# A fused decoder in float32 on one core: rotary attention's bank reads go ahead of the block turnings, and the second group's query weight sums go ahead of the last two rotations

## The reference

```python
def _L1_attn_ref(X, Wq, Wk, Wv, Wo):          # rotary, 16-wide heads
    Q = apply_rope((X @ Wq).reshape(Bs, Ts, H, dh))
    K = apply_rope((X @ Wk).reshape(Bs, Ts, Hkv, dh))
    V = (X @ Wv).reshape(Bs, Ts, Hkv, dh)
    ...
    scores = jnp.einsum('bkgtd,bksd->bkgts', Qh, Kh) / jnp.sqrt(jnp.float32(dh))
    scores = jnp.where(causal[None, None, None], scores, -jnp.inf)
    attn = jax.nn.softmax(scores, axis=-1)
    ...
    return out @ Wo

def _L0_xattn_ref(q, k, v, Wq, Wk, Wv, Wd):   # context attention; _L1_xattn_ref is alike
    queries = (q @ Wq.T).reshape(B, Sq, NHEADS, HEAD_DIM).transpose(0, 2, 1, 3)
    keys = (k @ Wk.T).reshape(B, Skv, KVHEADS, HEAD_DIM).transpose(0, 2, 1, 3)
    ...
    queries = _rope(queries)                   # x * cos + rot * sin
    keys = _rope(keys)
    ...
    attn = jax.nn.softmax(scores, axis=-1)
```

## Time and profile before

| | |
|---|---|
| time, median of 3 runs | 2554.17 us (2552.24 to 2556.07) |
| the profiled execution's own time | 2556.09 us |
| its span (first to last instruction) | 2554.8 us |
| mean granted clock of TensorE | 0.989 |
| busy: PE, PEld, DVE, ACT, POOL | 95%, 60%, 65%, 39%, 29% of the span |
| the chain that ended last, by engine | PE 80%, DVE 11%, ACT 2%, issue 2%, POOL 2%, DMA 2% |

### The profile page before, as it was taken

How to read it: one execution, slowest core, us unless ns; L and a number is a source line. 1 busy time by engine, 2 the same in 40 slices (tenths; PEclk the granted TensorE clock), 3 DMA queues, 4 the chain that set the end, 5 groups by cost and what they waited for, 6 DMA issues and landing times.

```text
span 2554.8 us, 37687 instructions
## 1 busy us (share of the span) xinstructions
PE 2436.9 (95%) x13016; PEld 1542.3 (60%) x13016; DVE 1671.0 (65%) x3133; ACT 989.5 (39%) x3580; POOL 733.7 (29%) x755
## 2 busy tenths in 40 slices
PE   8999999999999798999999999999998999999998
PEld 7865666666655565456666666556664554555554
DVE  3487777777755777677777777565665644445565
ACT  0013444444444366344444434433555412323330
POOL 1037344443322111364344443222221221000002
PEclk9999999999999999999999999999999999999999
DMA  8452233322322266121333222222661020214430
GB/s 177 101 139 73 76 96 99 87 79 79 93 77 83 91 199 200 62 94 60 95 99 98 89 75 79 87 95 86 191 189 61 22 75 30 95 66 153 132 100 33
DMA packets 220382, 249.97 MB, mean 98 GB/s; under 512 B 49792, under 2 KB 165952, under 8 KB 218144
## 3 DMA queue, kind: packets, MB, share of 16 engines
q1 hardware_dynamic: 212128, 218.20, 28.9%
q10 hardware_dynamic: 8064, 29.36, 3.0%
HBM read 161.49 MB, written 85.98 MB: 97 GB/s over the span
## 4 chain that ended last, share of the span: by engine, by line
PE 80%; DVE 11%; ACT 2%; issue 2%; POOL 2%; DMA 2%; SPq 0%; DVEq 0%; ACTq 0%; POOLq 0%
PE banks L752 12%; PE banks L840 12%; PE banks L824 4%; PE banks L902 4%; PE banks L868 3%; PE banks L303 3%; PE banks L720 3%; PE banks L2091 3%; PE banks L733 3%; PE banks L1521 3%; PE banks L2142 3%; PE banks L2431 2%; PE banks L2468 2%; PE banks L2119 2%; PE banks L2161 2%
## 5 line engine op out<-in xcount | busy, mean ns | idle before, releaser
L947 ACT ACTIVATE E_x<-S_x,sm_x 128x128 f32<-128x128 f32 x512 | 199.2, 390 | 304.3 <-DVE sm_x L1121 304.3
L1183 POOL TENSOR_TENSOR QT<-QT,const 128x512 f32<-128x512 f32 x128 | 171.7, 1342 | 427.7 <-DVE turned L1001 427.7
L161 POOL TENSOR_TENSOR norm_spread<-norm_mv,const 128x1 f32<-128x1 f32 x96 | 20.7, 216 | 909.3 <-DVE norm_mv L157 909.3
L752 PE MATMUL banks<-xT,weights 128*128 128x512 f32 x512 | 237.1, 597 | 7.6 <-POOL weights L1178 5.8
L2589 ACT ACTIVATE E_s<-banks,top_s 128x128 f32<-128x128 f32 x512 | 180.0, 379 | 95.8 <-DVE top_s L2696 95.8
L1079 DVE TENSOR_TENSOR x<-banks,x 128x256 f32<-128x256 f32 (+1 forms) x288 | 147.2, 511 | 84.6 <-PE banks L840 78.6
L840 PE MATMUL banks<-weights,OT 128*128 128x256 f32 x768 | 195.1, 384 | 6.3 <-DVE weights L1062 6.3
L840 PEld LDWEIGHTS banks<-weights,OT 128*128 128x128 f32 x768 | 142.8, 191 | 67.9 <-issue 27.9
L954 ACT ACTIVATE OT<-banks 128x512 f32<-128x512 f32 x128 | 76.1, 595 | 258.2 <-PE banks L902 258.2
L1185 POOL TENSOR_TENSOR QT<-QT,turned 128x512 f32<-128x512 f32 x128 | 169.0, 1320 | 10.0
L752 PEld LDWEIGHTS banks<-xT,weights 128*128 128x128 f32 x512 | 95.0, 191 | 116.5 <-issue 105.6
(11 more groups left out here) (320 smaller groups left out, 4908.1 us busy)
## 6 DMA issues: line engine op xcount, KB each, us to landing
scratch_pt<-blocks_x SPq DMA_DIRECT2D x124, 256.0 KB, 2.0
PT<-scratch_pt SPq DMA_DIRECT2D x496, 64.0 KB, 2.0
scratch_latent_pt<-blocks_s ACTq DMA_DIRECT2D x56, 512.0 KB, 3.6
PT_s<-scratch_latent_pt SPq DMA_DIRECT2D x224, 128.0 KB, 3.0
weights<-in_L_xwq SPq DMA_DIRECT2D x64, 256.0 KB, 3.9
weights<-in_L_xwo SPq DMA_DIRECT2D x64, 256.0 KB, 4.3
scratch_latent_pt<-blocks SPq DMA_DIRECT2D x30, 512.0 KB, 2.6
PT<-scratch_latent_pt SPq DMA_DIRECT2D x120, 128.0 KB, 3.0
```

The source lines that it names most:

```text
L752: mm = PE.matmul(to, left[:, k, head], moving, start=name in ("P1", "P2", "P4", "P5") and k == 0, stop=k == 1, skip_group_check=name in (" ...
L947: ins = AC.activation(head_of(e, j, u), scores_of(s, j, u), ACT.Exp, bias=sm[:, 0, j:j + 1], scale=1.0, accum_out=sm[:, 1, j:j + 1])
L1183: PO.tensor_tensor(four(to), four(to), spread(cos128, 4), ALU.mult).then_inc(*pool_step.one())
```

## The change

It has two parts.

In the context attentions, POOL makes the sums of group 1's query weights after six of the eight query rotations of group 0, ahead of the last two, where it had made them after all eight. The other groups are as they were.

In the rotary attention, VectorE's reads of the projection bank go ahead of `turn_blocks`. In rounds 1 the sine product comes first, then `turn_blocks`, then the addition to the queries (the function is split, `rope_queries`). In rounds 2 the wait for ScalarE's key copy and the reads of keys and values come first, then `turn_blocks`, then the turned keys. No instruction is added or taken away, and the queues of PE, ScalarE and SyncE keep their order.

```diff
--- before.py
+++ after.py
@@ -1190,13 +1190,11 @@
                         for i in range(2):
                             rope(NR * g + i, KT[g % 2][:, half_of(i)], False)
                         for m in range(8):
-                            if m == 5 and 1 <= g < G8 - 1:
+                            if m == (5 if g else 6) and g < G8 - 1:
                                 wq_sums(g + 1)
                             if m == 2 and 1 <= g and 8 * (g - 1) < 2 * pairs:
                                 wo_sums(g - 1)
                             rope(NR * g + 2 + m, query(g, *rotated(g)[m]), True)
-                        if g == 0:
-                            wq_sums(1)
                     for b in range(B):
                         norm.root(b)
 
@@ -2605,13 +2603,15 @@
                         if kind == "turn_q":
                             DV.wait_ge(*s_rq(b + 1))
                             DV.tensor_tensor(turned[:, :, :], four(work), spread(sin16, 4), ALU.mult).then_inc(*s_qsin.one())
-                            DV.wait_ge(*s_qsin(b + 1))
-                            DV.tensor_tensor(QT[b % 2][:, :, :], QT[b % 2][:, :, :], turned[:, :, :], ALU.add).then_inc(*s_roped.one())
                         if kind == "turn_k":
                             DV.wait_ge(*s_rk(b + 1))
                             DV.tensor_tensor(kturned[:, :], key_work(b)[:, 0:P], sin16, ALU.mult).then_inc(*s_ksin.one())
                             DV.wait_ge(*s_ksin(b + 1))
                             DV.tensor_tensor(KT[b % 2][:, 0, :], KT[b % 2][:, 0, :], kturned[:, :], ALU.add).then_inc(*s_k_here.one())
+
+                    def rope_queries(b):
+                        DV.wait_ge(*s_qsin(b + 1))
+                        DV.tensor_tensor(QT[b % 2][:, :, :], QT[b % 2][:, :, :], turned[:, :, :], ALU.add).then_inc(*s_roped.one())
 
                     def values(b, product, bias):
 
@@ -2680,6 +2680,7 @@
                         late_drain(0, "q")
                         late_drain(0, "k")
                         early_drain(0, "turn_q")
+                        rope_queries(0)
                         early_drain(0, "turn_k")
                     else:
                         then(DV.tensor_scalar(bias4[:, :], v["bq"], 0.25, None, ALU.mult))
@@ -2694,14 +2695,19 @@
                                 if s >= 2 and half == 0:
                                     DV.wait_ge(*s_exp(2 * s - 2))
                                 DV.tensor_reduce(top[s % 2][:, 4 * half:4 * half + 4].rearrange("p (a c) -> p a c", c=2), scores_of(s, half), AX.X, ALU.max, negate=True).then_inc(*s_top.one())
+                        if early(s)[0] == "turn_q":
+                            early_drain(early(s)[1], "turn_q")
+                        kind, at = late(s)
+                        if rotary and kind == "k":
+                            late_drain(at, kind)
                         if 1 <= s <= ROUNDS:
                             turn_blocks(s - 1)
-                        kind, at = late(s)
-                        if kind:
+                        if kind and not (rotary and kind == "k"):
                             late_drain(at, kind)
-                        kind, at = early(s)
-                        if kind:
-                            early_drain(at, kind)
+                        if early(s)[0] == "turn_q":
+                            rope_queries(early(s)[1])
+                        if early(s)[0] == "turn_k":
+                            early_drain(early(s)[1], "turn_k")
                         if scaled_at(s) is not None:
                             norm.scale(scaled_at(s))
                     norm.scale(B - 1)
```

## The result

The changed kernel takes 2564.35 us (median of 10 runs, 2558.81 to 2570.12), the kernel before 2556.36 us (median of 10 runs, 2552.24 to 2560.14). The ratio is 1.0031, with a 95% interval of 1.0021 to 1.0041, so the change costs 8.0 us, or 5.4 to 10.5. The forecast was 6.1 us more than before. It named 2560.3 us with a range of 2557.5 to 2563.5, which is 3.3 to 9.3 us over its base of 2554.17 us. Since the kernel before now has a median of 2556.36 us, the 8.0 us lie inside that range, while the bare time of 2564.35 us lies above it. The profiled execution of the changed kernel took 2563.9 us, its span is 2562.6 us and its mean granted clock 0.988 (before 0.989).

The account below looks back on a forecast made before the run. TensorE, busy 95% of the span, was taken to bound the kernel. Openings losing 5.1 us plus the rotary attention losing 1.0 made 6.1 us over the 2554.17 us base: 2560.3 us, range 2557.5 to 2563.5.

Parts of the forecast that it names:

- The mechanism of the openings: Context-attention openings: sums' wait goes, late rotations hold VectorE's sine products and step 0; P3 1.3 and 3.0 us later.
- I add 0.4 us for each attention: Context-attention openings: allowance for TensorE's products at half clock after the longer hole, 0.4 us in each.
- rival (d): Openings' delay is soaked up later in the stage by engines with slack; only 2 us remain, 2557 us; chance 0.13.
- block 0: Rotary attention: block of the round 1 kind turned 0.8 us later, costing 0.3 us, with ends of -0.4 and 0.8.
- block 25: Rotary attention: block of the round 2 kind turned later, lengthening TensorE's 1.71 us wait and costing the whole 1.5 us.
- the vanished waits for the sine product: Rotary rounds 1: seeming gain of 1.2 us in each of five rounds; ScalarE's copy moves by only 0.21 us.
- three rounds gain 0.27 us each: Rotary rounds 2: reads of keys and values start 0.27 us earlier, a gain in three of the rounds.
- rival (c): Lower clock holds for both products after both opening holes, and again behind block 0 or 25; 2565 us; chance 0.17.
- The wait of the key turn: Rotary rounds 2: TensorE's wait there grows from 0.4 to 1.3 us, as most of the saved time reappears.
- the other two DMA waits belong to blocks of rounds that don't change: Rotary attention: of TensorE's four waits for blocks returned by DMA, two were taken as unaffected, with no cost.
- (a): Openings: the last two rotations are not missed, so 7.5 us of wait and slow clock go; 2546 us; chance 0.07.
- (b): Openings lose, but the rotary attention gains 6.1 us from its five waits; about 2555 us; chance 0.13.

Follow-up runs that it names:

- part one alone: Kernel before with only the context attentions' weight sums moved ahead of the last two query rotations, rotary attention as before: 1.0032 of before, 8.2 us more.
- the sums after seven: Kernel before with the weight sums after seven of the eight query rotations, rotary attention as before: 1.0016 of before, 4.1 us more.
- three buffers: Kernel before with weight sums after six rotations and three buffers for the sine products instead of two, rotary attention as before: 0.9997 of before.
- rounds 1 alone: Kernel before with only the rotary attention's rounds 1 changed, sine product ahead of the block turning: 1.0001 of before.
- rounds 2 alone: Kernel before with only the rotary attention's rounds 2 changed, reads of keys and values ahead of the block turning: 1.0009 of before, 2.3 us more.
- part two alone: Kernel before with only the rotary attention changed, VectorE's bank reads ahead of the block turnings, context attentions as before: 1.0018 of before, 4.6 us more.
- four buffers alone: Kernel before with four buffers for the sine products instead of two, weight sums left late: 0.9998 of before.
- four buffers: Kernel before with weight sums after six rotations and four buffers for the sine products instead of two, rotary attention as before: 0.9973 of before, 6.9 us less.
- step 0 ahead of the keys: Kernel before with early weight sums and VectorE's rotations of group 1's keys behind step 0's reciprocal, rotary attention as before: 0.9982 of before, 4.6 us less.
- the kernel without blocks 0 and 25: Kernel before with VectorE's rotary bank reads ahead of the block turnings, except where blocks 0 and 25 are turned; context attentions as before: 1.0001 of before.

## Why the prediction was right, and where its terms were off

**The mechanism of the openings was right in every step.** In the changed kernel's trace no wait for line 1178 is left; VectorE idles ahead of both sine products; the eighth rotation ran from 216.86 to 219.46, its last instruction from 218.20 (forecast 217.6 to 218.9); the mask came at 221.58 (221.0), the addition at 222.90 (222.3), the reciprocal at 224.70 (224.1). Each is about 0.6 us late, of which 0.24 us is the later start of this trace and 0.3 us the slowed sums, which took 5.9 us and not 5.6 (208.38 to 214.28). The copy of P5 ran from 226.09 to 226.66.

**The size of one term was too small: "I add 0.4 us for each attention"** for the half clock. P3 came 2.1 us later in stage 1 and 3.8 us in stage 4 (starts less what the trace was late by), where 1.3 and 3.0 had been worked out from the copy. P6 took 3.57 us until P3 and so ended 0.55 us after the copy in both stages, and P3 itself lost another 0.2 and 0.8 us. In all 2.3 and 4.6 us, 6.9 where 5.1 was forecast. Of the 6.9 us the low clock has 2.1, where 0.8 had been put down for it, and the late copy 4.8, where it was 4.3. The low clock came in both openings, as in part one alone and with the sums after seven: six holes of 4.7 to 5.2 us, and P6 at the low clock six times. By the rule of the Trainium skill that the prediction named (TensorE: Matmul & The Clock Gate, What's actually happening) the default state is throttled and activity releases it; the trace agrees for these six, while behind the 2.17 and 1.72 us with three buffers P6 ran at the high clock.

**What was not in the sum: a later place gave 1.5 us back, by luck.** In group 2 of stage 1 TensorE waits for VectorE (L1062) in both kernels. Before, the products behind it ran at the low clock, after not:

```profile
271.07 2.07 PE L840 MATMUL banks<-weights,OT 128*128 128x256 f32 x4 [2.32 <-DVE weights L1062]
```

```profile
273.54 1.13 PE L840 MATMUL banks<-weights,OT 128*128 128x256 f32 x4 [2.22 <-DVE weights L1062]
```

The wait is nearly as long, so the clock differed. It isn't the change that does this. In the traces of rounds 1 alone and rounds 2 alone, whose context attention is that of the kernel before, this product took 1.13 us as well, and the place came 1.1 and 1.5 us earlier against the opening. So it doesn't show rival (d) either, that engines with slack soak the delay up.

The profiled pair came out at 7.8 us because 10.1 us of losses (6.9 in the openings, 3.2 in the rotary attention) met 1.5 us here and 1.2 us of clock in later stages that had nothing to do with the change. That the total lies so near the forecast of 6.1 us is in part luck.

**The rotary attention was forecast at +1.0 us, and cost 3.2 us in the trace and 4.6 [1.5, 7.7] us when alone.** By terms, in the one pair of traces: block 0 cost 0.3 us, as forecast, and block 25 cost 1.0 us instead of 1.5. But these waits scatter where nothing was changed, for block 0 from 2.24 to 3.67 us and for block 25 from 0.33 to 1.84 us. By the means given above (1.46 and 3.02 us) the wait for block 25 grew by 1.6 us, which bears the forecast of 1.5 us out. The term for block 0 can't be told from zero. That the vanished waits for the sine product are worth next to nothing was right (rounds 1 alone: no change). The forecast that three rounds gain 0.27 us each wasn't borne out: the second to the 25th product of probabilities took 119.5 us, before 119.4. With rounds 1 alone they took 118.1, so 0.3 us per sequence are there to be had, but the reads of rounds 2 bring nothing more (the last distance of the key turns is 20.97 us in the changed kernel). No term stood for the clock behind block 25; only rival (c) had it. In this pair of traces it seems to have cost 1.9 us (from block 25 to the end +2.9 us, of it 1.0 for the wait). It wasn't repeated: with part two alone and with rounds 2 alone the granted clock there was 0.83, as before. From the 25th to the 32nd product the three traces with rounds 2 changed took 33.4, 32.7 and 31.3 us, a mean of 32.5, and the eight with the rotary attention as before 30.1 to 32.7, a mean of 30.9. The means differ by the 1.6 us of the wait and no more, though the ranges overlap. Where the rest of the 4.6 us comes from, if it is there at all, stays open.

**Two statements were wrong without costing much.** The wait of the key turn was to grow from 0.4 to 1.3 us; it grew to 0.65 and 0.85, since the time first shows at the projection ahead of it (L2434 for ScalarE's copy, 0.58 us). And "the other two DMA waits belong to blocks of rounds that don't change" suggested that no others would come. There were four more, the largest of 1.51 us for the seventh block. They can't be put down to the change: with the rotary attention as before, part one alone shows 1.32 us for the eighth block and four buffers alone 0.61 us for the seventh.

**The rivals.** (a), that the two rotations aren't missed, is wrong for this kernel and right with four buffers: the openings are then 8.0 us shorter, where it had said 7.5. (b) is excluded by rounds 1 alone. (c) had the clock in the openings right and its price too high, since P3 would have waited for the copy during most of the slow P6.

## What to carry to other kernels

Before work is moved ahead of other work in a queue, look for who waits for the work moved back, and through which resource: here no product needed the two rotations, but a sine product needed the buffer that they read, and step 0 stood behind it in the same queue. Give the moved work a buffer of its own or move the waiting instruction too, and the same move gains: with two, three and four buffers the openings cost 6.9 us, nothing, and gained 8.0 us. And a wait that vanishes is worth only the idle time of the engine that comes next: 1.3 us of TensorE's waits were worth 0.3 us here.

## What the runs showed of the hardware

**A hole of the same length brings the clock down in one execution and not in the next.** TensorE's wait for the weight sums in stage 4 is followed by P5. In two kernels that don't differ there:

```profile
1109.64 1.98 PE L752 MATMUL banks<-xT,weights 128*128 128x512 f32 x4 [2.71 <-POOL weights L1178]
```

```profile
1108.29 2.56 PE L752 MATMUL banks<-xT,weights 128*128 128x512 f32 x4 [2.74 <-POOL weights L1178]
1110.65 3.04 PE L752 MATMUL banks<-weights 128*128 128x512 f32 x4
```

The first is part two alone, the second rounds 2 alone; this opening took 9.03 and 10.74 us. Behind 2.17 us (three buffers) the clock stayed up, behind 2.21 us (step 0 ahead of the keys) the next product took 2.51 us. In stage 1 the same wait, 3.16 us long, was followed by P5 in 3.78 us and P6 in 3.12 us in the kernel without blocks 0 and 25, so that its opening took 12.46 us where the same instructions took 11.13 before.

**That goes with much of the scatter between runs.** The 10 runs of the changed kernel go from 2558.81 us at a mean granted clock of 0.990 to 2570.12 us at 0.986, and one at 0.985 took 2566.18. In the experiments each kernel's runs lie in a range of 0.3 to 0.7%, and its shorter ones mostly have the higher clock. On the third chip the kernel before had a mean clock of 0.9889 over its runs and the highest median, on the first two 0.9895 and 0.9899. So even with 7 to 12 runs of a kernel against 30 or more the intervals here are some 0.1% to each side, and one profile of each isn't enough: the part of the trace in question must be compared, with its own clock.

**GpSimd and VectorE slow each other when both work on SBUF tiles.** GpSimd's addition on 128x512 took 1.26 us where VectorE was idle or read a PSUM bank (218.20 us, changed kernel) and 1.59 us beside VectorE's sine product from `QT` (209.47 us, kernel before). That half of a sine product took 1.66 us; the same from a PSUM bank took 0.68 us with GpSimd busy (217.00, above). The Trainium skill (Trainium Architecture — The Big Picture, What this means for kernel authors) says that these two engines share a port pair which one of them locks; the trace agrees in that both get slower, and doesn't show which of them holds the ports.
